# Layer 1 of a two-layer adaLN network: causal zeroing moved from matrix products to GpSimd, VectorE operations moved or fused, and the extra work of all engines placed at other steps

## The reference, cut to what matters

```
x  = x + gate0 * y0                      # the rest of layer 0: expert rows, gathered
h  = layernorm(x) * (1 + scale) + shift
q, k, v = split(h @ w_in)                # 16 heads of 8
s  = q k^T / sqrt(8) + bias(i - j)       # attention a=0
o  = softmax(s) v
a, g = split(o @ w_gate + b_gate)
x  = x + gate1 * a * sigmoid(g)
h  = layernorm(x) * (1 + scale) + shift
h2 = rmsnorm(h) * g1                     # latent attention, causal, a=1
lat = h2 @ Wdkv;  q, k, v = h2 @ Wq, lat @ Wuk, lat @ Wuv
s  = where(j <= i, q k^T / sqrt(8), -1e9)
h  = h + softmax(s) v @ Wo
... top-2 of 8 experts on rmsnorm(h), added to x
```

## Time and profile before

| | us |
|---|---|
| median of 3 runs (lowest, highest) | 1846.85 (1842.99, 1851.0) |
| the profiled execution, its own time | 1861.73 |
| its span (first to last instruction) | 1860.0 |
| TensorE busy | 1617.7 (87%) |
| VectorE busy | 1326.5 (71%) |
| ScalarE busy | 1007.1 (54%) |
| GpSimd busy | 779.3 (42%) |
| mean granted TensorE clock | 0.95 |

### The profile page before, as it was taken

One profiled execution on the slowest core, in us unless ns is written; L12 is line 12 of the kernel. 1 busy time (PEld: TensorE's weight loads), 2 busy tenths in 40 slices (PEclk: granted clock), 3 DMA queues, 4 the chain that ended last, 5 costly groups with the idle time before them and its releaser, 6 DMA issues.

```text
span 1860.0 us, 50554 instructions
## 1 busy us (share of the span) xinstructions
PE 1617.7 (87%) x19264; PEld 1179.7 (63%) x19264; DVE 1326.5 (71%) x4176; ACT 1007.1 (54%) x2196; POOL 779.3 (42%) x1021
## 2 busy tenths in 40 slices
PE   3899898899883939989999999989999988888887
PEld 2677676777772727766666666656767766544545
DVE  6678777876761127788778798897886786685646
ACT  1545454455451316665666667666666656564532
POOL 3111311220115237786656566565464574243210
PEclk7899999999995969999999999999999999988999
DMA  3631122122004424344423325143452333535321
GB/s 111 190 94 46 40 84 65 36 69 82 5 7 122 157 81 155 131 151 151 160 64 128 125 84 164 56 147 98 131 161 88 114 127 111 161 98 162 109 62 53
DMA packets 143839, 194.53 MB, mean 105 GB/s; under 512 B 21920, under 2 KB 110176, under 8 KB 142320
## 3 DMA queue, kind: packets, MB, share of 16 engines
q1 hardware_dynamic: 129312, 171.75, 29.6%
q0 software_dynamic: 5760, 14.03, 2.4%
q10 hardware_dynamic: 8528, 5.51, 1.0%
HBM read 142.39 MB, written 50.69 MB: 104 GB/s over the span
## 4 chain that ended last, share of the span: by engine, by line
PE 44%; DVE 9%; issue 7%; ACT 5%; DMA 1%; POOL 1%; SPq 0%; another core or an unknown queue 0%; ACTq 0%; POOLq 0%; DVEq 0%
PE ps L2350 9%; PE ps L2333 7%; PE ps L2384 6%; PE ps L2394 3%; DVE l_XY L2601 3%; PE ps L2361 3%; ACT PT L2162 2%; PE ps L1229 2%; PE ps L2484 2%; PE ps L1238 2%; PE ps L2459 2%; PE ps L2410 2%; DVE ps L2601 1%; PE ps L2431 1%; PE ps L2522 1%
## 5 line engine op out<-in xcount | busy, mean ns | idle before, releaser
L2053 POOL TENSOR_SCALAR l_XY<-l_XY,l_nmax 128x512 f32<-128x512 f32 x512 | 374.9, 737 | 295.9 <-DVE l_nmax L2601 287.6
L2601 DVE CUSTOM_DVE_ANT_0 l_XY<-ps,strips 128x512 f32<-128x512 f32 x512 | 347.7, 687 | 170.4 <-PE ps L2333 115.2
L2162 ACT ACTIVATE PT<-ps 128x512 f32<-128x512 f32 x512 | 307.3, 601 | 248.0 <-PE ps L2350 236.3
L2333 PE MATMUL ps<-l_stack 72*128 72x512 bf16 (+3 forms) x1024 | 350.9, 348 | 50.1 <-DVE l_nmax L2601 35.5
L2350 PE MATMUL ps<-ident,l_XY 128*128 128x128 f32 x2048 | 320.6, 279 | 1.7 <-ACT PT L2162 1.4
L2350 PEld LDWEIGHTS ps<-ident,l_XY 128*128 128x128 f32 x2048 | 236.9, 142 | 91.0 <-issue 56.8
L2601 DVE CUSTOM_DVE_ANT_0 ps<-ps,mask 128x384 f32<-128x384 f32 (+3 forms) x512 | 250.2, 496 | 24.3 <-PE ps L2333 20.2
L2361 PE MATMUL ps<-l_stack 75*128 75x256 bf16 (+3 forms) x512 | 157.2, 308 | 22.0 <-ACT PT_odd L2165 7.5
L2333 PEld LDWEIGHTS ps<-l_stack 72*128 72x128 bf16 x1024 | 101.1, 99 | 100.5 <-DVE l_nmax L2601 55.7
L2384 PE MATMUL ps<-PT,v_aug 128*10 128x128 f32 x4096 | 137.6, 275 | 6.8 <-ACT l_O_sb L2171 6.4
L2165 ACT ACTIVATE PT_even<-ps 128x512 f32<-128x512 f32 (+1 forms) x256 | 125.1, 494 | 22.8 <-PE ps L2363 17.3
(11 more groups left out here) (372 smaller groups left out, 3215.9 us busy)
## 6 DMA issues: line engine op xcount, KB each, us to landing
l_stack<-parts_dram SPq DMA_DIRECT2D x384, 96.0 KB
strips<-bias_dram SPq DMA_DIRECT2D x16, 1792.0 KB
stack<-parts_dram SPq DMA_DIRECT2D x48, 384.0 KB
w_own<-table_dram SPq DMA_DIRECT2D x60, 256.0 KB
parts_dram<-l_parts SPq DMA_DIRECT2D x32, 384.0 KB
rows_dram<-mask SPq DMA_DIRECT2D x6, 2048.0 KB, 8.9
parts_dram<-parts SPq DMA_DIRECT2D x16, 384.0 KB, 6.5
x_b<-rows_dram SPq DMA_DIRECT2D x72, 64.0 KB
```

The costliest lines, as they stand in the source:

```text
L2053: nc.gpsimd.tensor_scalar(XY[:, c % XY_BUFS], XY[:, c % XY_BUFS], -1.0, nmax[:, c % 8:c % 8 + 1], ALU.mult, ALU.add).then_inc(y_pool, 1)
L2162: nc.scalar.activation(PT[:, u % QUADS, j], src.rearrange("p (k q) -> p k q", q=P), ACT.Exp).then_inc(moved, 1)
L2333: nc.tensor.matmul(ps[:, n % 3, 0:w], stack[0:STACK, 0, h, q * P:(q + 1) * P], stack[0:STACK, 1, h, 0:w], start=True, stop=True).then_inc( ...
L2601: nc.vector.tensor_tensor_reduce(out=dst, in0=src, in1=add, scale=-1.0, scalar=3.0e38, op0=ALU.add, op1=ALU.min, accum_out=low).then_inc(s ...
```

## The change

1. The mask product of `scores_turned` and its constant are gone. A new `causal(u)` on GpSimd sets the first 128 columns of all four heads of unit u to zero above the diagonal, after the exponential, in `PT_even` or `PT_odd`; `values_turned` waits for that.
2. Both additions to x (L2668, L2698) go to GpSimd (`x_added`, `x_gated`), for batch 0's first excepted.
3. `split`: VectorE's subtraction writes the second bfloat16 part at once; GpSimd repeats the subtraction in float32 (`first_less`) ahead of `last_part`. The cast is left only for batch 0 of attention 0.
4. In `mid`, `normalised`, times scale, plus shift (4 + 1 + 1 operations) become 4 + 4 fused ones: (x - mean) * scale, then h * rstd + shift.
5. Nearly all step numbers of the extras change (tables below), the plan of a group is spread over six stages, and SyncE waits for a store's landing ahead of the first load that reads it; that load of attention 1 is issued three steps later than before.

```diff
+MID = dict(product=23, sum=26, add=26, statistics=28, var=31, power=32, norm=33, norm2=37, square=41, square_var=42, square_power=44, xn=45, turn=46, split0=51, split1=53, less0=51, last0=56, less1=59, last1=59, store=62)
+LAST_MID = dict(product=23, sum=25, add=27, statistics=29, ..., split0=48, split1=53, less0=51, last0=51, less1=55, last1=55, store=57)
+PRE = dict(y0=-11, y1=-2, x=-1, statistics=4, var=9, power=10, xn=11, split0=24, split1=27, less0=29, last0=35, less1=37, last1=39, store=44)
-MIXED_STAGES = dict(wo=1, add=3, square=5, var=8, power=9, scale=15, turn=17, logits=19, top0=21, top1=25, both=25, gap=27, count=28,
-                    place=37, gates=37, scatter=38, plan=(50, 52, 54, 56, 58), fold=41)
+MIXED_STAGES = dict(wo=3, add=5, square=9, var=12, power=12, scale=15, turn=17, logits=19, top0=21, top1=25, both=25, gap=27, count=26, place=36, gates=36, scatter=37, plan=(47, 49, 57, 61, 63, 66), fold=41)
-SCATTER_EVERY = {0: 2, 1: 2, 2: 2, 3: 2, 4: 4, 5: 1}
+SCATTER_EVERY = {0: 4, 1: 4, 2: 4, 3: 4, 4: 3, 5: 1}
...
-PAIR_WINDOWS = ((0, MOE_START[1] + 68, 12, 8), (1, MOE_START[3] + 68, 12, 4), (2, MOE_START[5] + 46, 12, 3))
+PAIR_WINDOWS = ((0, MOE_START[1] + 76, 12, 8), (1, MOE_START[3] + 71, 12, 4), (2, MOE_START[5] + 44, 12, 3))
...
-GATHER_AT = 40
+PRE_GATHERS, MID_GATES = (45, 46, 49, 50), (19, 20)
...
-    steps += [(LATE + GROUP * k - 10 - (4 if k >= 27 else 0), 1, k) for k in range(4 * B)]
+    steps += [(LATE + GROUP * k - (7 if k % 4 == 0 else 10 + (4 if k >= 27 else 0)), 1, k) for k in range(4 * B)]
...
+def causal_at(m):
+    return [u for u in range(BIAS // 4) if turned_step(1, 4 * u + 3) + 2 == m]
...
@@ store_parts, stack_up
-                    sp.wait_ge(parts_stored, 32 * n + 32)
...
+                    if k % 4 == 0:
+                        sp.wait_ge(parts_stored, 32 * PART_NO[a, b] + 32)
...
@@ gpsimd
+                def causal(u):
+                    wait_moved(pool, ("T", (1, 4 * u + 3)))
+                    late = turned_keys(u % 4)[:, :, 0:P]
+                    nc.gpsimd.affine_select(out=late, in_=late, compare_op=ALU.is_ge, fill=0.0, base=0,
+                                            pattern=[[0, 4], [1, P]], channel_multiplier=-1).then_inc(masked, 1)
...
+                def x_added(b):
+                    pool.wait_ge(y_scaled, E + b)
+                    nc.gpsimd.tensor_tensor(x_rows(b), x_rows(b), y0[:], ALU.add).then_inc(x_in, 1)
+                def x_gated(b):
+                    pool.wait_ge(mid_sum, E + b + 1)
+                    nc.gpsimd.tensor_tensor(x_rows(b), x_rows(b), h_of(b), ALU.add).then_inc(x_mid, 1)
+                def first_less(k, a, b):
+                    pool.wait_ge(second_part, 2 * PART_NO[a, b] + k + 1)
+                    order.link(nc.gpsimd.tensor_tensor(qk[:, k, :], qk[:, k, :], parts[:, k, 0, :], ALU.subtract))
...
                 for m in range(STEPS):
+                    for b in range(1, B):
+                        if m == pre_step(b, "x"):
+                            x_added(b)
                     s, i = divmod(m, TILES)
+                    for u in causal_at(m):
+                        causal(u)
                     if 0 <= m - 1 < BIAS:
                         shift(m - 1)
...
@@ tensor: scores_turned, values_turned
                     nc.tensor.matmul(ps[:, to, 0:T - k * P], stack[:, 1, h, k * P:(k + 1) * P], stack[:, 0, h, k * P:T],
-                                     start=True, stop=False)
-                    nc.tensor.matmul(ps[:, to, 0:P], ident_b[:], mask_turned[:], start=False, stop=True).then_inc(turned, 1)
+                                     start=True, stop=True).then_inc(turned, 1)
...
-                    wait_moved(pe, ("T", (1, 4 * u + 3)))
+                    pe.wait_ge(masked, u + 1)
...
@@ vector: split, mid
+                        if PART_NO[a, b]:
+                            nc.vector.tensor_tensor(parts[:, k, 1, :], qk[:, k, :], parts[:, k, 0, :], ALU.subtract).then_inc(second_part, 1)
...
+                    if i == mid_of(b)["norm"]:
+                        dve.wait_ge(var_ready, VARIANCES[1, b] + 1)
+                        for t in range(TT):
+                            last = nc.vector.scalar_tensor_tensor(out=h[:, t, :], in0=x_tile(b, t), scalar=mean_var[1][:, t, 0:1],
+                                                                  in1=mid_rows[:, 2], op0=ALU.subtract, op1=ALU.mult)
+                        link(last)
+                    if i == mid_of(b)["norm2"]:
+                        linked()
+                        dve.wait_ge(rstd_ready, VARIANCES[1, b] + 1)
+                        for t in range(TT):
+                            last = nc.vector.scalar_tensor_tensor(out=h[:, t, :], in0=h[:, t, :], scalar=rstd[1][:, t:t + 1],
+                                                                  in1=mid_rows[:, 1], op0=ALU.mult, op1=ALU.add)
+                        last.then_inc(mid_rows_used, 1)
```

More of the change, by code:

```diff
@@ L1979, in _ @@
                             load_block_weights(n)
-                    if pre is not None and i == 30:
+                    if pre is not None and i == PRE["store"]:
                         store_parts(0, pre)
-                    if mid is not None and i == 57:
+                    if mid is not None and i == mid_of(mid)["store"]:
                         store_parts(1, mid)
@@ L1988, in _ @@
                         next_strips(s, i // GROUP + 1)
-                    if pre is not None and pre < B - 1 and i == 60:
+                    if pre is not None and pre < B - 1 and i == 20:
                         pre_row(pre + 1)
@@ new lines, in first_pre @@
+                def first_pre():
+                    scaled(0, 0)
+                    link(scaled(0, 1))
+                    linked()
+                    nc.vector.tensor_tensor(x_rows(0), x_rows(0), y0[:], ALU.add).then_inc(x_in, 1)
+                    dve.wait_ge(x_in, 1)
+                    statistics(0, 0)
+                    linked()
+                    variance(0)
+                    normalised(0, 0).then_inc(tok_ready, 1)
+                    for k in range(2):
+                        for part in range(2):
+                            split(k, 0, 0, part)
@@ L2677, in pre @@
                         wait_xn(("xp", b))
                         normalised(0, b).then_inc(tok_ready, 1)
-                    for at, k, part in ((22, 0, 0), (24, 0, 1), (26, 1, 0), (28, 1, 1)):
-                        if i == at:
-                            split(k, 0, b, part)
+                    for k in range(2):
+                        if m == pre_step(b, f"split{k}"):
+                            split(k, 0, b, 0)
                 def mid(b, i):
@@ L2715, in mid @@
                         dve.wait_ge(mid_squares, b + 1)
                         root_input(2)
-                    if i == 43:
+                    if i == mid_of(b)["xn"]:
                         dve.wait_ge(rstd_ready, VARIANCES[2, b] + 1)
                         nc.vector.tensor_tensor(xn[:], h, bc(rstd[2][:].unsqueeze(2), wide), ALU.mult).then_inc(tok_ready, 1)
-                    for at, k, part in ((49, 0, 0), (51, 0, 1), (53, 1, 0), (55, 1, 1)):
-                        if i == at:
-                            split(k, 1, b, part)
+                    for k in range(2):
+                        if i == mid_of(b)[f"split{k}"]:
+                            split(k, 1, b, 0)
@@ L2886, in router @@
                         gate_pair(b)
-                    if b == GROUPS[g][-1] and k in p["plan"]:
-                        plan_blocks(g, p["plan"].index(k))
+                    for step in range(len(p["plan"])):
+                        if b == GROUPS[g][-1] and k == p["plan"][step]:
+                            plan_blocks(g, step)
                 def block_product(n):
@@ L2958, in moe @@
                         nc.vector.tensor_tensor(x_rows(b), x_rows(b), h, ALU.add).then_inc(x_done, 1)
-                for i in range(30):
-                    pre(0, i)
+                first_pre()
                 dve.wait_ge(strips_loaded, 16 * STRIP_HEADS)
@@ L2969, in _ @@
                             divide(*what)
-                    if s in PRE_OF:
-                        pre(PRE_OF[s], i)
+                    for b in range(1, B):
+                        pre(b, m)
                     if s in MID_OF:
```

144 lines of the change are left out of this document (75 added, 69 removed).

## The result

| | before | after |
|---|---|---|
| median, 11 runs each, same chip (us) | 1849.53 | 1839.40 |
| lowest, highest | 1841.89, 1854.12 | 1832.73, 1842.31 |
| the profiled execution's own time | 1861.73 | 1839.8 |

The ratio is 0.9945, with an interval of 0.9925 to 0.9964. The change gains 10 us (0.55%) where I forecast 29. The direction was right and the size wrong by a factor of three; the time lies inside the range but near its upper end. The two profiled executions differ by 22 us: that of before is none of the 11 runs and longer than each of them, and 6.5 of the 22 arise ahead of the step loop, in layer 0, which the change does not touch (the loop starts at 693.2 us of the span before and at 686.7 after). The medians count.

What follows compares the result with a forecast made beforehand. The prediction took the kernel as mostly bound by TensorE, 0.72 of its busy time on the chain of waits. Terms -21 - 6 - 8 + 6 = -29 us gave 1833 us for the profiled execution, 1818 for the median; range 1785 to 1853.

Steps and rivals of the forecast that it cites:

- The mask products: 512 products leave TensorE's stream, 29.7 us, of which 0.72 lies on the path: -21 us, ends 0 and 29.7.
- The zeroing on GpSimd: 128 causal operations, 79 us of GpSimd time, hidden by about 3 us of slack: 0, or 26 us if uncovered.
- the port: GpSimd and VectorE block each other in SBUF: 3 us more on VectorE, below 1 on the path, within the +6.
- VectorE's relief: Casts, additions and fused norm take 32 us off VectorE, 0.18 of it on the path: -6 us, ends 0 and 26.
- Placement, its bursts and waits: Spreading the extras over other steps: -8 us, ends -10 and 18; GpSimd's bursts and VectorE's new waits: +6, ends 0 and 43.
- a gather of which the last part is issued three steps ahead, 4.6 us: VectorE's new wait for a gather, with 4.6 us allowed for it; costed only inside the +6 us for bursts and waits.
- SyncE: Attention 1's first load of a batch, behind attention 0's DMAs, lands just in time: 0, else 1 us per batch.
- The late stage: Sign of being wrong: the last 150 us no shorter than before while the main stage is.
- (b): Product time returns as TensorE's wait for VectorE; VectorE's 6 us paid by GpSimd's 6: 1843 to 1847 us; chance 0.18 with (d).
- (c): GpSimd becomes the bound at steps 45 to 62 and pushes back the transposes: 43 - 29 = +14, 1861 us; chance 0.14.
- (d): The zeroing is needed late and values_turned waits every time: +26 on -29, 1844 us; chance 0.18 with (b).
- (a): TensorE's bound is all there is and the spreading works: 59 us faster, 1788 us; chance 0.20.

Runs made afterwards that it cites:

- e1: The kernel before without its 512 mask products and nothing zeroed in their place; ratio 0.9947 to the kernel before, 9.9 us faster.
- e3: The changed kernel with nothing zeroed on GpSimd, so its output differs; ratio 0.9896 to the kernel before.
- e4: The changed kernel with the mask products back on TensorE and no zeroing on GpSimd; ratio 0.9949 to the kernel before.
- e2: The kernel before with mask products out and the zeroing on GpSimd in, all step numbers as before; ratio 1.0015 to the kernel before.
- e9: e1 plus 77 GpSimd selects up to step 470, on a buffer nobody reads, still waiting for ScalarE; ratio 0.9992 to the kernel before.
- e10: e9 with the selects no longer waiting for ScalarE; ratio 0.9986 to the kernel before.
- e11: e10 with a memset of the same buffer, which reads nothing, in place of each select; ratio 0.9944 to the kernel before.
- e5: The kernel before with VectorE's relief, six-stage plan and SyncE's moved wait; mask products and old steps stay; ratio 0.9978 to the kernel before, 4.1 us faster.
- e7: The changed kernel with the first half of the gathered rows' scaling, batches 2 and 3, at steps 60 and 124, not 53 and 117; ratio 0.9880 to before.
- e14: e12 with GpSimd's shift ahead of the zeroing and batch 0's first stack load 10 steps ahead, not 7; ratio 0.9871 to the kernel before.
- e12: The changed kernel with gathers, scaling and other early steps of batches 2 and 3 placed as for batch 1; ratio 0.9871 to the kernel before.
- e6: The changed kernel with the late stage's step numbers as in the kernel before; ratio 0.9950 to the kernel before.
- e13: e12 with the mask products back on TensorE and no zeroing on GpSimd; ratio 0.9923 to the kernel before.

## Why the prediction was wrong, step by step

- **The mask products, -21; measured -10** (e1), and -10 again in the new order (e3 against e4). The step that failed is "on the path by TensorE's share: 0.72 x 29.7". TensorE's work left the path there, and VectorE's took its place. The share of one chain is no price where a second is nearly as long. The earlier trace rows had the hint, in the 41.6 us for which TensorE waits for the maximum.
- **The zeroing on GpSimd, 0; measured +9 to +13** (e3 to after, e1 to e2). This step failed most. "I cost it at 0, hidden by these 3 us" asked only whether the zeroed values come in time. In the main stage they do, and in e9 nobody needs them, and the price is the same. What it costs is the port, which I had as "3 us more on VectorE, below 1 on the path". With 77 units VectorE was busy 6.6 us longer (e10), and nearly all of it was on the path, not 0.18 of it. That this is so because these selects meet VectorE in stretches where it is the bound is my reading; no run separates the stretches. The Trainium skill (SBUF — State Buffer, Who interferes with whom) says that a VectorE instruction with two SBUF inputs contends with a GpSimd instruction that reads SBUF, not with one that only writes it. e10 and e11 agree with both halves, 0.68 against 0.19 us. I had weighed the rule and priced it by a mean. Behind step 570 the values do come late. The waits of the change from 1547 to 1838 us have them:

```profile
PE ps L2448 <- POOL PT_even L2084: 6.0, 2, 3.2
PE ps L2448 <- POOL PT_odd L2084: 5.5, 3, 2.1
```

  These 11.5 us are hardly on the path: e3 has no such wait and is only 1 us shorter there (290.5 and 291.4 us by the steps).
- **VectorE's relief, -6; measured -4** (e5). The way of reckoning held. VectorE's sum fell by 20 us, not 32; about half of that gap (6 us) is the fused norm at 508 and 472 ns, where I took 394.
- **Placement, its bursts and waits, -8 and +6; measured -5 together** (e5 to e4). The sum is near, and both terms are wrong. In steps 144 to 480 the placement gains 18.5 us, my upper end: the earlier trace rows said it, and I halved it. The stretch after that answers to the second row:

```profile
1094.00:1122.00 28.00, 26.08 (x297) 17.72 (x295) 26.82 (x90) 18.90 (x43) 24.81 (x33) 1.00 0.36 118
```

  TensorE has 93% there, where it had 87%, as the forecast asked. What lost is one wait, "a gather of which the last part is issued three steps ahead, 4.6 us". I took 1.55 us per step, the main stage's mean. In steps 48 to 64 attention 1 has not begun and a step takes 16.0 / 16 = 1.0 us, so the gather had 3 us and needed 6.5. I had named this wait and left it in a lump of 6 with all others; alone it was 12 by the ratios of e7, of which the profiles place 6.
- **SyncE, 0; some 2 us by one wait.** I had it landing just in time. In the change TensorE waits once for a load of attention 1, the first of all, at 851 us:

```profile
PE ps L2388 <- DMA l_stack<-parts_dram: 1.8, 1, 1.8
```

  In e14, where that load has its old step, the wait isn't there, and the time is that of e12: it is too small to measure. For the other batches no run has the old step in the new order, but none of their loads is waited for in this way.
- **The late stage.** From step 512 to the end the change takes 5.5 us more than before (291.2 and 285.7). The sum had no term for it, though the forecast named it as a sign of being wrong. Its step numbers are not the cause as far as e6 can tell, and neither is the zeroing, since e4 does without it and has 292.4. It is there with the relief alone (e5, 290.8), and not in the profiles of the two kernels with `shift` first (284.1 and 285.4), whose medians don't show it. The granted clock is lower from 1560 to 1700 us (0.85, before 0.89), but over the whole of this stretch kernels with the same 0.91 take from 281.1 to 293.0 us (e1, e13). By what way it comes stays open.
- **The rivals.** (b), that the time comes back as a wait, is what happened to the products, and its time was the nearest. (c) had the right engine in the wrong way: GpSimd isn't the bound; it holds up VectorE, and VectorE TensorE. Of (d), which at 1844 us was nearly as near as (b), the waits of `values_turned` are there in the late stage alone, and e9 has the price without them. (a) fell.

Summed anew from the runs: products -10, zeroing +10, relief -4, placement -5 (with the early wait of +12 in it). That is -9 for the 10 measured. That the time fell inside the stated range is luck: two terms were wrong by 10 us and more.

## What to carry to other kernels

Of an operation moved to an idle engine ask who waits for it, and also whom it stops while it runs: a GpSimd operation that reads SBUF held VectorE's two-input work for its full length where the two met (0.68 us in place of 0.19), and one that only writes did not. It is not charged everywhere: the 77 selects of e10 ran for 55 us and cost 7. Where two engines are nearly level, a saving on one is worth the slack to the other, not one chain's share. Give each new wait on a transfer a term of its own, with the step length of the stage in which it stands.

## What the runs showed of the hardware

The memset, free for two-input work, is not free for VectorE's norm of 128x128 (one tensor in, float32). From 840 to 1560 us, in e1, e10 and e11:

```profile
L2631 DVE TENSOR_SCALAR l_xn<-x_sb,l_mean_var,l_rstd 128x128 f32<-128x128 f32 x44 | 17.0, 449 | 0.0
```
```profile
L2649 DVE TENSOR_SCALAR l_xn<-x_sb,l_mean_var,l_rstd 128x128 f32<-128x128 f32 x44 | 20.8, 535 | 0.0
```
```profile
L2648 DVE TENSOR_SCALAR l_xn<-x_sb,l_mean_var,l_rstd 128x128 f32<-128x128 f32 x44 | 20.4, 607 | 0.0
```

Both lengthen it, the memset no less than the select (means of 607 and 535 ns, 20.4 and 20.8 us busy). In e11 such a norm takes 0.33 us where nothing of GpSimd runs beside it, and 0.43 to 0.62 beside the memset alone. The 3.4 us of this group did not show in the time of e11; VectorE's busy time as a whole has 0.8 of them in steps 144 to 480.
